# Reading the first two condition entries from DRAM into registers in an AdaLN feed-forward kernel

## The reference

```python
W = weights[condition]                       # 16 x 64 x 64, picked by 64 entries
y = einsum('bct,bcd->bdt', x, W)             # x: 64 x 64 x 1024
w = (unpack6(qweight) - zero_point) * scale  # 1024 x 1024 from 6-bit fields
out = x + einsum('bsk,nk->bsn', y, w) + bias
```

## Time and profile before

| | |
|---|---|
| median of 3 executions | 286.14 us (286.12 to 287.18) |
| the profiled execution's own time | 285.89 us |
| its span, first to last instruction | 283.9 us |
| PE busy, share of the span | 98% |
| DVE, ACT, POOL busy | 66%, 30%, 34% |
| DMA moved | 39.48 MB, mean 139 GB/s |
| share of the chain that ended last: PE, DMA, ACT | 96%, 2%, 1% |

### The profile page before, as it was taken

The page is one execution under the profiler, slowest core; times in us unless marked ns, Lnnn a source line. Parts: engine busy times, 40 slices in busy tenths (PEclk is TensorE's granted clock), DMA queues, the critical chain, the costliest instruction groups (busy, mean ns, idle before and its releaser), DMA issues.

```text
span 283.9 us, 8490 instructions
## 1 busy us (share of the span) xinstructions
PE 277.6 (98%) x3307; PEld 231.8 (82%) x3307; DVE 186.1 (66%) x255; ACT 83.9 (30%) x169; POOL 95.4 (34%) x38
## 2 busy tenths in 40 slices
PE   8999999899999999999999999999999999999995
PEld 3888888788888888988888888888888888888885
DVE  3776886785566566865559555676667655595554
ACT  3786323342044300633017310443106330060000
POOL 0008602964430444314442444404443044430000
PEclk9999999999999999999999999999999999999999
DMA  7992571456114541345114551144413552101112
GB/s 278 398 306 81 161 240 65 152 159 230 74 74 157 160 179 66 115 163 195 74 74 124 167 208 74 74 155 157 154 70 117 166 195 95 74 37 74 74 74 74
DMA packets 20685, 39.48 MB, mean 139 GB/s; under 512 B 6850, under 2 KB 7106, under 8 KB 20674
## 3 DMA queue, kind: packets, MB, share of 16 engines
q1 hardware_dynamic: 19730, 36.96, 37.3%
q10 hardware_dynamic: 944, 2.38, 2.3%
HBM read 22.54 MB, written 16.78 MB: 138 GB/s over the span
## 4 chain that ended last, share of the span: by engine, by line
PE 96%; DMA 2%; issue 1%; ACT 1%; DVE 0%; SPq 0%
PE o_ps L286 71%; PE y_ps L286 12%; PE y_ps L255 10%; DMA w_sb<-in_L_cond_weights_dram 1%; PE o_ps L255 1%; PE o_ps L268 0%; DMA ids<-in_itok_B_dram 0%; PE o_ps L297 0%; ACT qT L436 0%; PE y_ps L268 0%; SPq L155 0%; PE y_ps L297 0%; ACT y_hi L420 0%; DVE o_sb L607 0%; DVE o_sb L609 0%
## 5 line engine op out<-in xcount | busy, mean ns | idle before, releaser
L286 PE MATMUL o_ps<-qT,y_hi 128*128 128x512 f32 (+1 forms) x448 | 171.6, 386 | 0.2 <-ACT qT L436 0.2
L286 PE MATMUL o_ps<-qT,y_lo 128*128 128x512 f32 (+1 forms) x448 | 171.2, 385 | 0.0
L627 POOL TENSOR_TENSOR resid<-x_sb,bias_bc 128x1024 f32<-128x1024 f32 x32 | 94.7, 2968 | 154.9 <-DVE o_sb L534 134.1
L286 PEld LDWEIGHTS o_ps<-qT,y_hi 128*128 128x128 f32 x448 | 83.6, 188 | 17.4 <-ACT qT L436 0.4
L286 PEld LDWEIGHTS o_ps<-qT,y_lo 128*128 128x128 f32 x448 | 83.6, 188 | 16.8
L526 DVE TENSOR_TENSOR o_sb<-o_ps,scale_bc 128x512 f32<-128x512 f32 x54 | 37.3, 692 | 75.6 <-PE o_ps L286 75.6
L420 ACT ACTIVATE y_hi<-y_ps 128x512 fp32r<-128x512 f32 x56 | 29.4, 610 | 99.2 <-PE y_ps L255 98.8
L534 DVE TENSOR_TENSOR o_sb<-o_sb,resid 128x512 f32<-128x512 f32 x63 | 51.5, 823 | 1.9
L411 ACT ACTIVATE junk<-x_sb 128x1024 bf16<-128x1024 f32 x32 | 33.9, 1058 | 60.7 <-DMA x_sb<-in_x_dram 60.7
L515 DVE SCALAR_TENSOR_TENSOR resid<-zs_bc,ysum,resid 128x1024 f32<-128x1024 f32 x32 | 42.5, 1329 | 0.0
L505 DVE TENSOR_TENSOR y_lo<-y_ps,y_hi 128x512 fp32r<-128x512 f32 x57 | 35.7, 684 | 6.6 <-ACT y_hi L420 6.6
(11 more groups left out here) (35 smaller groups left out, 64.0 us busy)
## 6 DMA issues: line engine op xcount, KB each, us to landing
x_sb<-in_x_dram SPq DMA_DIRECT2D x32, 512.0 KB, 3.3
out_dram<-o_sb SPq DMA_DIRECT2D x63, 256.0 KB, 2.1
q_raw<-in_L_ffn_qweight_dram ACTq DMA_DIRECT2D x6, 384.0 KB, 5.3
w_sb<-in_L_cond_weights_dram SPq DMA_DIRECT2D x63, 16.0 KB, 2.0
q_raw<-in_L_ffn_qweight_dram SPq DMA_DIRECT2D x2, 384.0 KB, 6.3
scale_bc<-_L_ffn_weight_scale_dram SPq DMA_DIRECT2D x1, 512.0 KB, 5.8
zs_bc<-n_weight_zero_point_dram SPq DMA_DIRECT2D x1, 512.0 KB, 5.9
bias_bc<-in_L_ffn_bias_dram SPq DMA_DIRECT2D x1, 512.0 KB, 6.6
```

Of the source, the lines that this page charges most:

```text
L286: last = nc.tensor.matmul(bank, part[:, slot, kt, :], qT[:, kt, col:col + width], start=(kt == 0 and part is y_hi), stop=(kt == KT - 1 and ...
L627: nc.gpsimd.tensor_tensor(resid[:, j % RING, :], x_sb[:, j % RING, :], bias_bc[:], ALU.add).then_inc(xbias_ready, 1)
```

## The change

Tile 0's two entries no longer come from the list in SBUF. SP and ACT each load theirs from the list in DRAM into a register (`pick_first`, at a fixed place, with no bounds given), with no wait ahead of it. SP's first transfer is now x of tile 0; the list's transfer into SBUF is issued behind tile 0's first matrix, x of tile 1 follows it, and the wait for the list stands behind x of tile 1, ahead of the picks for tile 1. On ACT the pick and the second matrix move ahead of the one-element activation.

```diff
+        cond_row = cond.rearrange("(a b) -> a b", a=1)
+
         def pick(eng, at):
             return eng.value_load(ids[0:1, bass.ds(at, 1)], min_val=0, max_val=NCOND - 1)
+
+        def pick_first(eng, half):
+
+            return eng.value_load(cond_row[0:1, half:half + 1])
...
-            sp.dma_start(ids[:], cond.rearrange("(a b) -> a b", a=1)).then_inc(ids_loaded, 16)
             load_x(0, 0)
+            load_w_half(sp, 0, 0, pick_first(sp, 0))
+            sp.dma_start(ids[:], cond_row).then_inc(ids_loaded, 16)
+            load_x(1, 0)
             sp.wait_ge(ids_loaded, 16)
-            load_w_half(sp, 0, 0, pick(sp, 0))
-            load_x(1, 0)
             load_w(1, 0)
             for n in (4, 6):
                 load_q(sp, n)
...
             for n in range(2):
                 load_q(act, n)
+            load_w_half(act, 0, 1, pick_first(act, 1))
             act.wait_ge(warm_ready, 1)
             nc.scalar.activation(junk[:, 1, 0:1], warm[:, 0:1], ACT.Copy)
-            act.wait_ge(ids_loaded, 16)
-            load_w_half(act, 0, 1, pick(act, 1))
             for n in (2, 3, 5, 7):
                 load_q(act, n)
             place_q(0)
```

## The result

The median went from 286.54 us (6 runs of the kernel before, beside the new one) to **290.42 us**; the ratio is 1.0136, with a 95% interval of 1.0105 to 1.0167. The forecast was 286.4 with a range up to 287.8: it was wrong, the change costs 1.4%.

What follows compares the result with a forecast made beforehand. PE was taken to bound the kernel, busy 277.6 of 283.9 us, so only the start could move. Terms 0 + 0.15 + 0.1 + 0 = 0.25 us on 286.14 gave 286.4 us, range 285.8 to 287.8.

Steps and rivals of the forecast that it cites:

- part 1: Reads of tile 0's entries on SP and ACT: 1.2 us each, matrices issued at 2.35 and 2.85.
- third rival: ACT's DRAM read is slow, over 2.2 us, and holds up block 2: 0.95 us, 287.2 us; chance 0.08.
- Rivals 1: x of tile 1 overtakes block 2, which lands up to 1.28 us later: 1.2 us, 287.3 us; chance 0.15.
- Part 2: Mix of tile 0: the earlier matrix gains 0 to 0.09 us, booked as 0.
- Part 3: x of tile 0 issued together with block 0 delays the mix of tile 0: 0.15 us, between 0 and 0.8.
- Part 4: List behind the matrix: tile 1's matrices issued 1.6 us later, cost at its mix 0.1 us, between 0 and 1.65.
- rival 2: SP's wait for the list delays tile 1's second matrix; PE idles 1.65 us at its mix, 288.0 us; chance 0.15.
- Part 5: ACT's table load and one-element activation follow the matrix, ending near 5.1, with 0.95 us of cover: cost 0.

Runs made afterwards that it cites:

- runs without reads: Changed kernel with entry 0 as a constant for tile 0's two batches, so no register is loaded; the first, in the changed kernel's transfer order: ratio 1.006.
- list-first order: Changed kernel with entry 0 as a constant for tile 0, and SP issuing the list ahead of x of tile 0: ratio 1.0027.
- best order: Changed kernel with entry 0 constant for tile 0, list issued first, and x of tile 1 issued behind tile 1's matrices: ratio 0.9972.
- warm PE: Changed kernel with 12 instead of 9 matmuls on zeros at the start and 5 more between the transposes of blocks 1 and 2: ratio 1.0117.
- x of tile 1 late: Changed kernel with x of tile 1 issued behind tile 1's matrices: ratio 1.0103.
- matrix-first run without reads: Changed kernel with entry 0 constant for tile 0, and SP issuing tile 0's matrix ahead of x of tile 0, the list behind both: ratio 1.0068.
- kernel before with x late: Kernel before, with x of tile 1 issued behind tile 1's matrices: ratio 1.0009.
- two with a single reader: Changed kernel with only ACT reading its entry from DRAM (ratio 1.0127), or only SP (1.0214); the list is issued first and the other picks from SBUF.
- three of the repairs above: Changed kernel with block 2 ahead of ACT's read (1.0155), extra matmuls on zeros (1.0117), or x of tile 1 behind tile 1's matrices (1.0103).

## Why the prediction was wrong

The median came out at 290.42 us against a forecast of 286.4. The step that failed is **part 1, the read at 1.2 us**. I took it from the ids transfer and thought of one trip to DRAM; it was two in a row, and together they took 3.7 us. The ends of my own bounds, 0.26 to 3.57 us, nearly held it, but I carried only the middle into the sum. Of the two figures of the Trainium skill that I had beside it (Runtime: NRT & Kernel Launch), the 1.3 us of "The launch sequence" and the 200 ns for each register, which stand under "Instruction fetch mechanics", neither comes near the 3.7 us measured. The matrices were to be issued at 2.35 and 2.85 and went out at 5.01 and 5.60. At 3.7 us the third rival decides, since its limit was 2.2.

**Rival 3, the slow read**, had the mechanism and the place: block 2 behind ACT's read. It was given 0.08 and 0.95 us. Its price failed on three points. Block 2 was issued 2.76 us late, where the rival had counted 1 us as free of charge; it then took 4.5 us instead of 3.0, because x of tile 1, issued 0.09 us ahead, went first (1.3 us, shown by moving it); and PE, idle 2.40 us, ran at the lower clock afterwards (1.1 us, shown by filling the hole). Rivals 1 and 3 were priced as alternatives, and here they came together, with the clock as a third that no rival had. By the rows: 2.76 + 0.5 is the 3.25 us of block 2, and with about 1 us of clock that is the 4.2 us at the mix of tile 1. Two of the sums on record were not carried through either: 286.4 and 0.95 are 287.35 for rival 3, not 287.2, and 286.4 and 1.2 are 287.6 for rival 1, not 287.3. Neither would have changed the range.

**Rival 1, x of tile 1 overtaking block 2**, was right in place and price in the changed kernel: 1.3 us at block 2. In the runs without reads the price was 1.4 us (7.52 against 8.96 in the list-first order), but the way was another: x did not go first, the two shared the engines and landed together, in two of them although block 2 had been issued first. Two transfers issued within 0.1 us of each other should have had more than 0.15.

**Part 2, no gain from an earlier matrix**, was right, and stronger than I put it: issued at 1.6 us without any read, the matrices let the mix start at 7.05, later than the 6.64 of before, and at 6.58 in the best order.

**Part 3, x beside block 0**: block 0 was unpacked 1.5 us later without reads and 1.6 in the changed kernel, more than my upper end of 1.28, and not because x went wholly first. The two shared, as I had assumed (from 2.6 to 4.4 us SP's queue had 53% of the engines' time and ACT's 41%), and landed 0.2 us apart; sharing alone was dearer than the half that I took. Its cost was still only 0.1 to 0.25 us at the mix of tile 0 (7.30 against 7.05 and 7.20 without reads), near the 0.15 booked.

**Part 4, the list behind the matrix**, booked 0.1 us, and no wait came, but not by its own strength. Without reads tile 1's matrices were issued at 8.11 and took 3.6 and 3.7 us, about as I had reckoned; the second landed at 12.39, 0.25 us past the 12.14 of before, and was covered because block 2 had put the mix at 13.51. In the changed kernel they were issued at 8.46 and 9.13 and took longer (the row of landings for both):

```profile
DMA to landing us min/median/max: 5.3/5.3/5.3
```

The second landed at 14.45, 2.3 us past 12.14. That is the place of **rival 2** and more than its price of 1.65 us; it stayed hidden only because block 2 and the clock had moved the mix to 16.36. That it cost nothing is luck.

**Part 5**: the table load moved to 6.19 and ended at 7.48, not at 5.1, so its cover was gone; ACT's first real work started at 8.29, after 0.61 us of waiting for its own queue. It cost nothing, since block 2 was later still, but I had not tied it to the length of the read.

## What to carry to other kernels

A load of one word from DRAM into a register blocks its queue for the address and the word in turn: price it from a run, under the load of the moment, and count everything that is issued behind it. Where the DMA engines have a backlog, ask which transfer stands ahead of which: issuing one sooner moves it only if it passes something, and it can push something back. Here the x transfer next to the weight block was worth 1.3 us at block 2, and the matrix that the chain names 0.06 at its mix. And do not take a gain at one point of the start for a gain at the end: follow it to the last instruction.

## What the runs showed of the hardware that I had not expected

Two transfers issued within 0.1 us of each other on SP's and ACT's queues were served one after the other in the changed kernel (x of tile 1 wholly first, 97.3% of the engines' time from 7.6 to 8.6 us) and side by side in the three runs without reads that have them together (56.1% and 42.2% from 6.6 to 7.6 us in the first). Block 2 lost 1.3 us in the one way and 1.4 us or more in the other. What decides between the two was not found; it is not the order of issue alone.

PE's hole in the mixes of tiles 2 and 3 (0.23 us before) follows a transfer of the queue named instruction, 16 KB each, and not the kernel's own waits. In the nine profiles that have the hole, PE went on 1.3 to 1.5 us after that packet ended: it ended at 21.68 before and PE resumed at 23.06; 24.13 and 25.42 without reads; 24.89 and 26.27 with the warm PE; 25.18 and 26.61 with x of tile 1 late. In the other five (the list-first and the matrix-first run without reads, the kernel before with x late, and the two with a single reader) PE came to that place only 1.6 to 2.2 us after the packet's end, and there was no hole; in the list-first run the same lag, 1.46 us, ends a hole of 0.70 us at 18.37 instead. The hole past 50 us is in all fourteen profiles, 0.92 to 1.65 us long, and ends 1.2 to 1.6 us after another such packet (49.16 and 50.50 before). The packet is in the view of DMA by queue of the run without reads, from 22.5 to 24.2 us (packets, MB, share):

```profile
q1 hardware_dynamic: 45, 0.13, 19.1%
q8 instruction: 1, 0.02, 3.5%
```

So about 1 us won in the start can be given back there, which is a good part of why three of the repairs above moved the mix of tile 1 by 1.1, 1.4 and 1.9 us and the end by 0.0, 0.3 and 0.3. No run moved these packets on purpose, so that they are the cause is read from their timing and not shown; what sets the time of a packet, the backlog of transfers or PE's own progress, was not tested.
